# A bf16 copy of the layer-norm input, its loads on the POOL queue, and a fifth weight slot

## The reference, cut to what matters

```python
def reference(x, input_weights, xis, proj_matrix, w1, s1, w2, s2, h1, hs1, h2, hs2, w3, s3):
    # x: (4, 4096, 1024) f32; 16384 tokens, 2048 for each core
    xn = (x - mean(x)) / sqrt(var(x) + 1e-5)                # layer norm over the 1024 features
    # random features: rfs(v) = exp(ab*(proj_matrix @ v) - 0.5*|v|^2*ab^2) * exp(xis) / 32, ab = xis
    s = rfs(xn) @ rfs(input_weights).T                      # (tokens, 1024)
    h = silu(xn @ w1.T * s1) * (xn @ w2.T * s2)             # w1, w2: 4096 x 1024
    h = gelu(h @ h1.T * hs1)                                # 4096 x 4096
    h = gelu(h @ h2.T * hs2)                                # 4096 x 4096
    g = silu(h @ w3.T * s3)                                 # 1024 x 4096
    return x + s * g
```

## Time and profile before

| | |
|---|---|
| median of the runs | 2779.48 us (2 runs, 2779.43 to 2779.54) |
| the profiled execution's own time | 2779.54 us |
| its span, slowest core | 2778.0 us |
| spans of the 8 cores | 2773.7 to 2778.0 us |
| granted TensorE clock, mean of each core | 0.984 to 0.985 |
| TensorE busy | 2651.2 us, 95% |
| DMA | 400.44 MB, 144 GB/s |

### The profile page before, as it was taken

The page is one execution under the profiler, slowest core; times in us unless marked ns, Lnnn a source line. Parts: engine busy times, 40 slices in busy tenths (PEclk is TensorE's granted clock), DMA queues, the critical chain, the costliest instruction groups (busy, mean ns, idle before and its releaser), DMA issues.

```text
span 2778.0 us, 28292 instructions; the slowest of 8 cores (2773.7 to 2778.0 us)
## 1 busy us (share of the span) xinstructions
PE 2651.2 (95%) x12086; PEld 1185.9 (43%) x12086; DVE 259.9 (9%) x382; ACT 358.3 (13%) x496; POOL 188.5 (7%) x359
## 2 busy tenths in 40 slices
PE   2799999999999999999999999999999999999995
PEld 0344444444444444444444444444444444444442
DVE  2223100000023300000002310000002200000001
ACT  0212101010121111010111200101012111010100
POOL 0000000000000000000000000000000000000000
PEclk9899999999999999999999999999999999999997
DMA  9158999999989899999988899999998899999994
GB/s 153 35 87 124 156 153 153 152 152 153 148 151 161 128 153 153 153 152 153 153 138 170 124 155 153 148 157 153 153 145 153 133 159 153 152 153 152 152 153 88
DMA packets 67115, 400.44 MB, mean 144 GB/s; under 512 B 7328, under 2 KB 7600, under 8 KB 21936
## 3 DMA queue, kind: packets, MB, share of 16 engines
q0 software_dynamic: 52800, 373.32, 87.3%
q1 hardware_dynamic: 14192, 25.31, 3.7%
HBM read 763.51 MB, written 8.39 MB: 278 GB/s over the span
## 4 chain that ended last, share of the span: by engine, by line
PE 95%; DMA 2%; DVE 1%; ACT 1%; issue 0%; DVEq 0%; SPq 0%; POOL 0%; ACTq 0%; POOLq 0%
PE pb L474 64%; PE pb L501 8%; PE pb L382 8%; PE pb L405 8%; PE pb L359 2%; PE pb L435 2%; DMA g_sb<-iwT 1%; PE pb L333 1%; PE pb L243 1%; DMA xt_r<-xT 1%; ACT t L514 0%; PE pb L245 0%; DVE h_sb L297 0%; DVE feats L234 0%; DVE ln_tmp L280 0%
## 5 line engine op out<-in xcount | busy, mean ns | idle before, releaser
L474 PE MATMUL pb<-h_sb,wring 128*128 128x512 bf16 x4096 | 884.7, 379 | 0.0
L474 PE MATMUL pb<-g_sb,wring 128*128 128x512 bf16 x4096 | 884.7, 379 | 0.0
L474 PEld LDWEIGHTS pb<-h_sb,wring 128*128 128x128 bf16 x4096 | 400.5, 98 | 484.8 <-issue 2.3
L474 PEld LDWEIGHTS pb<-g_sb,wring 128*128 128x128 bf16 x4096 | 400.8, 98 | 483.3
L501 PE MATMUL pb<-h_sb,wring 128*128 128x512 bf16 x1024 | 232.5, 391 | 18.8 <-ACT t L514 18.8
L382 PE MATMUL pb<-xn_fm,wring 128*128 128x512 bf16 x1024 | 231.5, 379 | 0.0
L405 PE MATMUL pb<-xn_fm,wring 128*128 128x512 bf16 x1024 | 231.5, 379 | 0.0
L521 DVE TENSOR_TENSOR s_sb<-t,s_sb 128x512 f32<-128x512 bf16 x32 | 22.2, 692 | 1972.0 <-ACT t L514 1969.2
L485 ACT ACTIVATE h_sb<-pb,h2s_c 128x512 bf16<-128x512 f32 x128 | 88.0, 687 | 796.1 <-PE pb L474 786.9
L485 ACT ACTIVATE g_sb<-pb,h1s_c 128x512 bf16<-128x512 f32 x128 | 88.0, 687 | 692.9 <-PE pb L474 683.7
L501 PEld LDWEIGHTS pb<-h_sb,wring 128*128 128x128 bf16 x1024 | 102.3, 100 | 148.5 <-issue 34.3
(11 more groups left out here) (70 smaller groups left out, 389.5 us busy)
## 6 DMA issues: line engine op xcount, KB each, us to landing
wring<-h1p POOLq DMA_DIRECT2D x128, 1024.0 KB, 10.7
wring<-h2p POOLq DMA_DIRECT2D x128, 1024.0 KB, 10.6
wring<-w1p POOLq DMA_DIRECT2D x32, 1024.0 KB, 11.0
wring<-w2p POOLq DMA_DIRECT2D x32, 1024.0 KB, 14.0
wring<-w3p POOLq DMA_DIRECT2D x32, 1024.0 KB, 10.4
xt_sweep<-xT SPq DMA_DIRECT2D x32, 256.0 KB, 18.5
xt_r<-xT SPq DMA_DIRECT2D x32, 256.0 KB, 5.7
y<-s_sb SPq DMA_DIRECT2D x32, 256.0 KB, 5.1
```

The costliest lines, as they stand in the source:

```text
L474: ii = t.matmul(p[quad[og]][:, :], wring[:, slot, k8, og * 128:(og + 1) * 128], src_sb[:, kk * 8 + k8, :], start=(kk == 0 and k8 == 0), st ...
```

## The change

The tile `xt_sweep` becomes bf16. Its loads go out from POOL instead of SP (a load that casts has to), with the same guard, now waited for on POOL. The sum of x on PE takes bf16 operands (`ones_b` in place of `ones_c`). The weight ring gets a fifth slot; `xt_sweep` gives up 8 KB on each partition and the slot takes 8 KB. At the start the eight loads of sweep 0 stand in the program behind `projT` and `iwT`, and ahead of the xis row and the first ring loads. The other readers of `xt_sweep` (L234, L280) are left as they are and read bf16.

```diff
-        xt_sweep = sb("xt_sweep", [128, 8, TS], F32)
+        xt_sweep = sb("xt_sweep", [128, 8, TS], BF16)
...
-        wring = sb("wring", [128, 4, 8, TS], BF16)
+        wring = sb("wring", [128, 5, 8, TS], BF16)
...
-        d_xts = Ctr(nc, stack, "d_xts", sy)
+        d_xts = Ctr(nc, stack, "d_xts", g)
...
-        d_wr = [Ctr(nc, stack, f"d_wr{i}", g) for i in range(4)]
+        d_wr = [Ctr(nc, stack, f"d_wr{i}", g) for i in range(5)]
...
         def emit_xts_loads(s_):
-            need(sy, cV, xts_state["guard"])
+            need(g, cV, xts_state["guard"])
             for j in range(8):
-                sy.dma_start(xt_sweep[:, j, :],
-                             xT[j * 128:(j + 1) * 128, s_ * TS:(s_ + 1) * TS])\
+                g.dma_start(xt_sweep[:, j, :],
+                            xT[j * 128:(j + 1) * 128, s_ * TS:(s_ + 1) * TS])\
                     .then_inc(d_xts.sem, 16)
...
-        slot_last = [0, 0, 0, 0]
+        slot_last = [0, 0, 0, 0, 0]
...
-            slot = ring_seq % 4
+            slot = ring_seq % 5
...
-                t.matmul(p[6][0:1, :], ones_c[:, 0:1], xt_sweep[:, j, :],
+                t.matmul(p[6][0:1, :], ones_b[:, 0:1], xt_sweep[:, j, :],
                          start=(j == 0), stop=(j == 7))
```

## The result

The changed kernel takes 2746.3 us against 2779.4 us (medians; ratio 0.988, 95% interval 0.987 to 0.989). It is 1.2% faster, which at a bound of 2% counts as no change, as forecast; 2744.7 us had been predicted, and the gain is 33.1 us instead of 34.8. The time lies 1.6 us from the forecast and inside its range. That it is so close is partly luck: the start gave some 6 us less than forecast, and the clock gave back about 5 us that no term of the sum had.

A forecast was written before the change was run, and what follows sets the result against it. The prediction took TensorE to bound the kernel, busy 2651.2 of 2778.0 us. Savings of 15.3 (steady blocks), 14.4 (start) and 5.1 us (first block), 34.8 in all, took 2779.5 to 2744.7 us; range 2735 to 2760 us.

The forecast's parts named there:

- PE bounds the kernel, the ring never stalls it: Whole kernel: TensorE busy 2651.2 of 2778.0 us and never waiting for ring loads, so a fifth slot gains nothing.
- Part 1, the steady blocks: Statistics block preparing sweeps 1 to 3: L243 in bf16 takes it from 10.4 to 5.3 us, saving 15.3 in all.
- The rival without clock loss: Steady statistics blocks: low clock came from the slow f32 stream, not the gap; 5.4 us more saved, 2739 us; chance 0.17.
- Part 2, iwT lands earlier: Program start: with xt_sweep queued behind it, iwT lands near 31 us, not 43.5; statistics start 14.4 us earlier.
- the bound of 10.7 us: First sweep's xt_sweep loads: if halved packets each cost what f32 ones cost, they take 10.7 us, landing at 41.6.
- The worst bound: Start: something other than shared engines paces iwT, landing at 43.5; xt_sweep at 50.2 to 54.2; 2 us saved.
- Squares in bf16: VectorE at the start: L234 takes 425 ns each, eight take 4.1 us, not 6.26; L280 keeps 687 ns.
- The first block: First statistics block, at the start with PE cold: 5.1 us instead of 10.18, saving 5.1; bounds 3.3 and 6.7.
- Part 3, the move to POOL: Later xt_sweep loads in POOL's queue ahead of strip 3's w1: cost nothing, hidden by strips 0 to 2 and L435.
- The slower rival: POOL's queue: strip 3's ring loads come late behind xt_sweep and PE stalls; 2808 us if xt_sweep takes 50; chance 0.03.
- The sum: Whole kernel: 15.3 us from steady blocks, 14.4 from the start and 5.1 from the first block, 34.8 saved.

## Why the prediction was right, point by point

- **PE bounds the kernel, the ring never stalls it.** Right. The fifth slot is worth nothing measurable (2743.4 us without it).
- **Part 1, the steady blocks.** Right in mechanism: the f32 matmul costs four bf16 passes, the gap of 2.0 us stays, the low clock stays in two of three blocks. Forecast 15.3 us, measured 17.1: the second block kept its clock. The rival without clock loss put the low stretch down to the slow f32 stream; that is out, since two blocks of bf16 lose the same 1.7 us. Its time came true in one block only.
- **Part 2, iwT lands earlier.** The mechanism is right: the order of the line decides, and putting `xt_sweep` first brings back the old landing. The size is wrong: 7.6 us instead of 14.4. Two things went into the miss. The first is a step left out: the prediction looked at who waits behind the moved loads on POOL, but not at who had been waiting behind them on SP. The `xt_r` loads had; set free, they cost iwT 4 to 5 us. The second is the rate. I took 157 GB/s for queue 0; with `xt_r` held, iwT lands at about 32 us, within 1 us of the forecast, but `xt_sweep` then needs another 8.5 us and not 6.7, so DVE waits for it (2.15 us in the row above). That lies halfway to the bound of 10.7 us, in which each packet costs what the f32 ones cost. The worst bound was also summed wrongly: it let `xt_sweep` land as late as 54.2 us, and then took the statistics from the 50.2, to start at 54.4. From 54.2 they would start at about 58.3, 2 us later than before instead of 2 us earlier. Nothing measured came near it.
- **Squares in bf16.** 425 ns were worked out for L234; the trace has 8 in 4.13 us, and 424 to 426 ns each. L280 stayed at 687 ns.
- **The first block.** Right. Forecast 5.1 us long and 5.1 us saved; measured 5.1 to 6.1 us over the eight cores against 10.1 to 11.1 before, 5.0 us saved by the means. The 4.0 us of the table compare two different cores. PE starts the block at half rate, which is read from its rows and not from the granted clock: the column shows 1.00 for the whole block, while the starts lie 0.43 us apart up to 53.9 us and 0.21 to 0.22 us behind that:

```profile
49.23 0.63 PE L245 MATMUL pb<-feats,ones_b 128*1 128x512 bf16 x1
49.66 0.63 PE L243 MATMUL pb<-xt_sweep,ones_b 128*1 128x512 bf16 x1
...
54.56 0.38 PE L243 MATMUL pb<-xt_sweep,ones_b 128*1 128x512 bf16 x1
54.77 0.38 PE L245 MATMUL pb<-feats,ones_b 128*1 128x512 bf16 x1
```

- **Part 3, the move to POOL.** Right: in sweep 1 the sixth ring load is issued 11.1 us after the sweep's first L382, the delay that the fifth load had before (814.23 us in the earlier trace rows, with the first L382 at 803.17), and the eight loads follow it:

```profile
784.94 3.62 PE L382 MATMUL pb<-xn_fm,wring 128*128 128x512 bf16 x16
```

```profile
796.00 0.53 POOL L222 DMA_DIRECT2D wring<-w2p  x1 [25.37 <-DVE h_sb L419]
796.52 4.24 POOL L161 DMA_DIRECT2D xt_sweep<-xT  x8
800.70 0.59 POOL L222 DMA_DIRECT2D wring<-w1p  x1
```

  The slower rival did not show. Of the starvation that the Trainium skill warns of ("SBUF — State Buffer", section "SBUF: two separate sides") no run here shows anything: the eight issues take 4.24 us, with DVE at work on L419 beside them, against 4.29 at the start, and their loads land after 14.7 us (median), sooner than the 18.5 of before. Whether L419 uses both ports no run here shows, so the warning is not tested. The loads of w1, one of which now stands behind them in each sweep, land after 14.2 us instead of 11.0; strips 0 to 2 hide it.
- **The sum.** 34.8 us forecast, 33.1 measured. By the means over the cores, the way to the first statistics gave 7.2 us less than forecast and the first block 0.1 less; the stretch behind it gave 1.2 that were in no term, the steady blocks 1.9 more, and the w3 strips 3.0 that were in no term. The last two are clock that came back and that nothing in the sum foresaw. So the total is closer than its parts deserve, and that is luck.

**What stays open.** In these stretches the clock falls only behind a gap, but a gap does not always bring the fall: the second block keeps its clock after a gap of 2.0 us like the others'. It does so in five kernels whose starts differ by up to 18 us (blocks of 5.2, 3.5 and 5.2 us in the changed kernel, with four slots, with either order of the start, and with `xt_r` held). It loses it again when the blocks are made longer, and the third block keeps its clock too when the gaps in w3 are gone. So neither the time since the start nor the length of the gap settles it. What does, no run here tells. The same holds for the w3 strips: their 3.0 us are a higher granted clock behind the same 4.7 us gap, but why the clock is higher is not shown.

## What to carry to other kernels

When loads are moved from one queue to another, follow both queues: the one they join, and the one they leave, where whatever stood behind them now runs earlier and may take the engines from the transfer that the start waits for. At the start of a program, order the loads by their first reader; here that was worth as much as taking the f32 passes out of two blocks. And look for short waits of PE on a bank guard before anything else: two changes of bank numbers, which move no data, won 10.7 and 29 us alone. In the kernel that has both the four sweeps are 36 us shorter, more than the whole change studied won.

## What the runs showed of the hardware that I had not expected

- Gaps of 2.0 us on PE can cost about as much again in clock: 1.7 us, in three blocks out of three before, in two of the changed kernel, in one when the gaps in w3 are gone. Gaps of 4.7 us cost 1.3 to 2.7 us on top. Without either the granted clock stays at 1.00 in these stretches.
- Two f32 loads of 256 KB each, beside a cast load of 2 MB written, delayed it by 4 to 5 us, while at the 196 GB/s of that queue before they account for 2.7 us.
- The eight cast loads of 1.05 MB in rows of 1 KB take 7.5 to 9.4 us behind other casts (the rows of DVE above, from the landing of iwT to that of `xt_sweep`), 110 to 140 GB/s written, where the casts with longer rows ran at some 150.
